# Seven of sixteen heads: the cap of the attention bias as a factor on GpSimd instead of identity products on TensorE

## The reference, cut to what matters

```
slopes = 2 ** (-0.5 * (h + 1))                     # h = 0..15
rel = pos[:, None] - pos[None, :]                  # query minus key
bias = minimum(rel * slopes[h], 8.0)
scores = einsum('bhqd,bhkd->bhqk', q, k) * 8 ** -0.5 + bias
probs = softmax(scores, axis=-1)
out = einsum('bhqk,bhkd->bhqd', probs, v)
```

## Time and profile before

| | us |
|---|---|
| median of 3 runs | 986.8 |
| lowest, highest | 986.79, 990.37 |
| profiled execution | 988.53 |
| span of the profiled execution, first to last instruction | 986.5 |

### The profile page before, as it was taken

How to read it: one execution, slowest core, us unless ns; L and a number is a source line. 1 busy time by engine, 2 the same in 40 slices (tenths; PEclk the granted TensorE clock), 3 DMA queues, 4 the chain that set the end, 5 groups by cost and what they waited for, 6 DMA issues and landing times.

```text
span 986.5 us, 19021 instructions
## 1 busy us (share of the span) xinstructions
PE 783.2 (79%) x5641; PEld 564.8 (57%) x5641; DVE 549.3 (56%) x2190; ACT 395.9 (40%) x947; POOL 357.9 (36%) x543
## 2 busy tenths in 40 slices
PE   0798479999999999952489999999999982038894
PEld 0676355555666677742246676667666651028883
DVE  4688573233322332333588989898987714026672
ACT  0456121222212322210036666766676661025562
POOL 5000517777850134433222423242322102744552
PEclk9999668999999999986569999999999995559997
DMA  9970001111100132303654444444443014111110
GB/s 250 155 221 0 0 1 36 40 41 41 44 0 14 52 112 78 96 30 90 128 106 95 90 108 93 102 83 106 95 85 67 3 45 155 54 53 55 50 50 14
DMA packets 75114, 72.44 MB, mean 73 GB/s; under 512 B 8125, under 2 KB 65680, under 8 KB 72732
## 3 DMA queue, kind: packets, MB, share of 16 engines
q1 hardware_dynamic: 69436, 60.38, 27.3%
q0 software_dynamic: 5600, 11.12, 3.5%
HBM read 43.71 MB, written 27.33 MB: 72 GB/s over the span
## 4 chain that ended last, share of the span: by engine, by line
PE 52%; DVE 18%; issue 12%; DMA 5%; POOL 5%; ACT 3%; DVEq 2%; SPq 2%; POOLq 0%; ACTq 0%
PE bank L1475 10%; PE bank L1476 9%; DVE rt L1065 6%; PE bank L1498 6%; PE bank L1527 4%; PE bank L1617 3%; PE bank L1569 3%; POOL sorted_rows L766 3%; PE bank L1604 3%; PE bank L1599 2%; DMA arena<-arena 2%; SPq L548 1%; DVEq L1180 1%; PE bank L1435 1%; PE bank L1707 1%
## 5 line engine op out<-in xcount | busy, mean ns | idle before, releaser
L1065 DVE CUSTOM_DVE_ANT_0 rt<-bank,alibi 128x256 f32<-128x256 f32 x512 | 192.9, 419 | 44.4 <-PE bank L1569 37.5
L973 DVE TENSOR_TENSOR arena<-arena,bank 128x512 f32<-128x512 f32 (+1 forms) x128 | 75.0, 587 | 187.8 <-ACT arena L1253 187.8
L1280 ACT ACTIVATE arena<-bank 128x512 f32<-128x512 f32 x256 | 150.6, 598 | 55.4 <-PE bank L1604 49.5
L1253 ACT ACTIVATE arena<-bank 128x512 f32<-128x512 f32 (+1 forms) x128 | 66.1, 517 | 202.9 <-PE bank L1476 202.9
L1569 PE MATMUL bank<-arena 72*128 72x256 bf16 x512 | 104.7, 289 | 26.6 <-DMA arena<-qk_parts 13.4
L1599 PE MATMUL bank<-arena 81*128 81x256 bf16 x512 | 117.0, 274 | 8.3 <-ACT arena L1280 4.7
L1475 PE MATMUL bank<-arena 128*128 128x320 f32 (+2 forms) x256 | 115.7, 534 | 7.5 <-DVE arena L973 7.5
L1476 PE MATMUL bank<-arena 128*128 128x320 f32 (+2 forms) x256 | 111.9, 519 | 0.0
L1604 PE MATMUL bank<-arena,ident_b 128*128 128x256 bf16 (+8 forms) x544 | 80.2, 243 | 0.0
L1569 PEld LDWEIGHTS bank<-arena 72*128 72x128 bf16 x512 | 39.0, 102 | 69.4 <-DVE arena L1065 42.8
L1475 PEld LDWEIGHTS bank<-arena 128*128 128x128 f32 x256 | 42.8, 193 | 53.5 <-DVE arena L973 41.1
(11 more groups left out here) (242 smaller groups left out, 1402.9 us busy)
## 6 DMA issues: line engine op xcount, KB each, us to landing
arena<-qk_parts SPq DMA_DIRECT2D x48, 192.0 KB
arena<-qk_parts SPq DMA_DIRECT2D x144, 64.0 KB
qk_parts<-arena SPq DMA_DIRECT2D x16, 384.0 KB, 2.8
back_rows<-empty_row SPq DMA_DIRECT2D x1, 4096.0 KB, 37.8
arena<-back_rows SPq DMA_DIRECT2D x16, 256.0 KB, 3.8
arena<-in_w SPq DMA_DIRECT2D x2, 2048.0 KB, 10.9
xg_rows<-empty_row SPq DMA_DIRECT2D x1, 2580.0 KB, 38.5
arena<-xg_rows SPq DMA_DIRECT2D x8, 322.5 KB, 4.0
```

The source lines that it names most:

```text
L973: nc.vector.tensor_tensor(out, sil[:, k, 0:out.shape[1]], bank[4 + k][:, 0:out.shape[1]], ALU.mult).then_inc(hid_done, 1)
L1065: last = nc.vector.tensor_tensor_reduce(biased[n % 2 * QT + u], bank[n % 2][:, SEQ * u:SEQ * u + SEQ], alibi[:, h, P * (1 - u):P * (1 - u) ...
L1253: nc.scalar.activation(sil[:, k, 0:width], bank[2 + k][:, 0:width], ACT.Silu).then_inc(sil_done, 1)
L1280: nc.scalar.activation(prT3[:, n % (2 * HG)].rearrange("p k t -> p (k t)"), bank[2 + n % 2][:], ACT.Exp).then_inc(exp3_done, 1)
```

## The change

Three things change.

- FULL falls from 4 to 2. Heads 2 to 8 now take their linear bias from the contraction rows, and nothing is added by TensorE for their cap. Instead a table `factor` holds exp(min(8 - slope * rel, 0)) for them, and GpSimd multiplies the exponentials in `prT3` by it (`apply_factor`), from the column `capped_from(h, k)` on. The table is made once: GpSimd writes the corrections, and ScalarE takes the exponential of 128x1792 of it in one instruction ahead of its slot loop.
- `weigh` waits also for `factored` and moves from offset 28 to 30 (WEIGH), its copy from 29 to 31 (KEEP). All that follows on it moves by two slots, with small shifts of single steps. The ring `prT3` grows from 8 to 12 heads.
- GpSimd gets a slot loop. `combine` moves one slot ahead, from -41 and -40 to -42 and -41.

```diff
-FULL = 4
+FULL = 2
+PR = 3 * HG
-COMBINE_0, COMBINE_1, ... = -41, -40, ...
+COMBINE_0, COMBINE_1, ... = -42, -41, ...
-BACK = NH - 1 + EXP_LAG + 5
+FACTOR, WEIGH, KEEP = EXP_LAG + 2, EXP_LAG + 5, EXP_LAG + 6
+BACK = NH - 1 + WEIGH + 2
-RESIDUAL, RESIDUAL_STATS, RESIDUAL_VARIANCE = BACK + 14, BACK + 15, BACK + 19
-NORM_5, TURN_5, COPY_5, ROUTER_5, LOGITS_5 = BACK + 22, BACK + 27, BACK + 28, BACK + 30, BACK + 31
-ROOT_LAG = 5
+RESIDUAL, RESIDUAL_STATS, RESIDUAL_VARIANCE = BACK + 13, BACK + 15, BACK + 20
+ROOT, PARTS_QK, OUTPUT_BIAS, ROOT_5 = VARIANCE + 1, QK_COPY + 1, NORM + 13, BACK + 21
+NORM_5, TURN_5, COPY_5, ROUTER_5, LOGITS_5 = BACK + 24, BACK + 26, BACK + 27, BACK + 29, BACK + 30
...
+def capped_from(h, k):
+    return min((P * k + int(MAX_BIAS / SLOPES[h]) + 1) // 2 * 2, SEQ)
...
+            for h in range(FULL, CLAMPED):
+                f = factor[:, h - FULL, :]
+                strip(nc.gpsimd.tensor_scalar(f, rel[:, P:P + SEQ], -SLOPES[h], MAX_BIAS, ALU.mult, ALU.add))
+                strip(nc.gpsimd.tensor_scalar(f, f, 0.0, None, ALU.min))
...
+        def apply_factor(n):
+            c, h = divmod(n, NH)
+            pool.wait_ge(exp3_done, n + 1)
+            if n == FULL:
+                pool.wait_ge(factor_set, 1)
+            for k in range(QT):
+                first = capped_from(h, k)
+                if first < SEQ:
+                    pr = prT3[:, n % PR, k, first:SEQ]
+                    last = nc.gpsimd.tensor_tensor(pr, pr, factor[:, h - FULL, first - P * k:SEQ - P * k], ALU.mult)
+            last.then_inc(factored, 1)
...
+        act.wait_ge(rows_set, 1)
+        nc.scalar.activation(factor..., factor..., ACT.Exp).then_inc(factor_set, 1)
...
             for k in range(QT):
-                first = bias_from(h, k) if h < CLAMPED else SEQ
-                biases = range(BIAS_PARTS[h]) if first < SEQ else ()
+                biases = range(BIAS_PARTS[h]) if h < FULL else ()
...
         def weigh(g):
             pe.wait_ge(exp3_done, HG * (g + 1))
+            if k * HG < CLAMPED:
+                pe.wait_ge(factored, factors_to(HG * g + HG - 1))
```

More of the change, by code:

```diff
@@ L82, with factors_to @@
 SLOPE_PARTS = [bf16_parts(s) for s in SLOPES]
[L83 to L89, removed]
+BIAS_PARTS = [len([v for v in SLOPE_PARTS[h] if v]) for h in range(FULL)]
+STRIP = [sum(BIAS_PARTS[:h]) for h in range(FULL)]
+FACTORS = CLAMPED - FULL
+def capped_from(h, k):
+    return min((P * k + int(MAX_BIAS / SLOPES[h]) + 1) // 2 * 2, SEQ)
+def factors_to(n):
+    c, h = divmod(n, NH)
+    return FACTORS * c + min(max(h + 1 - FULL, 0), FACTORS)
 def batch_at(slot, offset):
@@ L276, in _build @@
     oT3 = carve([P, SEQ])
-    prT3 = carve([P, 2 * HG, QT, SEQ])
+    prT3 = carve([P, PR, QT, SEQ])
     bn5 = carve([P, 2, QT, 6])
@@ L284, in _build @@
     strip_a = carve([P, sum(BIAS_PARTS[:FULL]), SEQ + P], BF16)
-    strip_b = carve([P, sum(BIAS_PARTS[FULL:]), SEQ], BF16)
+    factor = carve([P, FACTORS, SEQ])
     rel = carve([P, SEQ + P])
@@ L387, in _build @@
     rows_set = sem("rows_set")
+    factor_set = sem("factor_set")
+    factored = sem("factored")
     rows_in = sem("rows_in")
@@ L752, in root5 @@
             nc.gpsimd.tensor_tensor(shift, shift, scale, ALU.mult).then_inc(rstd5_done, 1)
-        root(0)
-        for c in range(BATCH + ROOT_LAG):
-            if alive(c, BATCH):
+        def apply_factor(n):
+            c, h = divmod(n, NH)
+            pool.wait_ge(exp3_done, n + 1)
[7 more added lines that the diff above has]
+            last.then_inc(factored, 1)
+        for slot3 in range(FIRST_SLOT, LAST_SLOT):
+            n = head_at(slot3, FACTOR)
+            if n is not None and FULL <= n % NH < CLAMPED:
+                apply_factor(n)
+            if (c := batch_at(slot3, ROOT)) is not None:
+                root(c)
+            if (c := batch_at(slot3, PARTS_QK)) is not None:
                 parts(c)
-            if alive(c + 1, BATCH):
-                root(c + 1)
-            if alive(c, BATCH):
+            if (c := batch_at(slot3, OUTPUT_BIAS)) is not None:
                 output_bias(c)
-            if alive(c - ROOT_LAG, BATCH):
-                root5(c - ROOT_LAG)
+            if (c := batch_at(slot3, ROOT_5)) is not None:
+                root5(c)
         def send_sorted(i):
@@ L1333, in keep_logits @@
             nc.scalar.activation(lg5[:, QT * e:QT * e + QT, :].rearrange("p t e -> p (t e)"), bank[7][:, SEQ:SEQ + QT * E1], ACT.Copy).then_inc(lg5_done, 1)
+        act.wait_ge(rows_set, 1)
+        nc.scalar.activation(factor.rearrange("p h t -> p (h t)"), factor.rearrange("p h t -> p (h t)"), ACT.Exp).then_inc(factor_set, 1)
         for slot3 in range(FIRST_SLOT, LAST_SLOT):
@@ L1601, in score_turned @@
                 for a in biases:
-                    strip = (strip_a[:, STRIP[h] + a, P * (1 - k):P * (1 - k) + SEQ] if h < FULL else
-                             strip_b[:, STRIP[h] + a, first - P * k:SEQ - P * k])
-                    last = nc.tensor.matmul(out[:, first:SEQ], ident_b[:], strip, start=False, stop=(a == len(biases) - 1))
+                    last = nc.tensor.matmul(out, ident_b[:], strip_a[:, STRIP[h] + a, P * (1 - k):P * (1 - k) + SEQ],
+                                            start=False, stop=(a == len(biases) - 1))
             last.then_inc(st3_mm, 1)
```

36 lines of the change are left out of this document (14 added, 22 removed).

## The result

The changed kernel takes 1006.97 us (median; 1002.27 to 1010.32) where the kernel before took 988.50 on the same chip (986.79 to 990.37). The ratio is 1.0183, 95% interval 1.0134 to 1.0232: slower by 18.5 us, where 15 us less were forecast. The profiled execution had 1010.32 us, its span 1008.4, mean granted clock 0.889 (before 988.53, 986.5, 0.906).

What follows compares the result with a forecast made beforehand. TensorE and VectorE were taken as close to the limit, with a loop through the maxima's DMA setting the new period: 13 x (19.55 - 18.75) = 10.4 plus 5 from the tail, 15.4 us saved, 972 us forecast, range 958 to 983.

Steps and rivals of the forecast that it cites:

- Later steps by two slots: `weigh` and its followers two slots later: priced at nothing, since the slots in the drain are empty.
- The clock was named as a sign: TensorE's granted clock under 1.00 in the changed stage was listed as showing the forecast wrong; no time was given.
- Products removed: TensorE: 26 of 34 identity products in an entry go, cutting its own time by 1.9 us, 18.8 to 16.9.
- The tail: From entry 13 on, nothing is replicated and TensorE bounds; three entries save nearly 1.9 us each: 5 us.
- Combinations moved: VectorE: combination one slot earlier ends before GpSimd's `parts`, taking 1.0 us off VectorE, 18.3 to 17.3.
- GpSimd 12.1 us an entry: Twelve multiplications add 5.8 us to GpSimd's 6.3 in a period; not the bound.
- The heaviest head: GpSimd's multiplication for it takes 1.2 us against a 1.15 us slot, leaving `weigh` two slots to spare; wait costed at nothing.
- New contention: GpSimd's multiplications delay VectorE's normalisation by 0.4 to 0.7 us and maxima splits by 0.4, together 1.0 an entry.
- The loop through the DMA: Maxima queue behind `replicate`, landing 21.8 us after ScalarE's copy; two periods are at least 37.5 us, 18.75 each.
- Rival 3: Normalisation and splits each wait behind a full multiplication: 4.2 us, VectorE 21.5, time 1007; chance 0.10.
- the signs named for "wrong": No maxima wait with period under 18.2; splits and normalisation over 1.5 us more; TensorE waiting for GpSimd; clock under 1.00.

Runs made afterwards that it cites:

- the fifth buffer: The changed kernel with five buffers for VectorE's values instead of four, all offsets kept: 999.94 us, 1.0056 of the kernel before.
- The schedule alone: The kernel before with only the new offsets of `weigh` and its followers and the ring of 12; products kept, no factor, combination unmoved: 1012.95 us, 1.0194.
- Without GpSimd's work: The kernel before with the identity products of heads 2 to 8 left out and nothing in their place: 986.98 us, 0.9951.
- the run without GpSimd's work: The changed kernel with all multiplications on GpSimd left out, GpSimd signalling at once: 1006.61 us, 1.0157 of the kernel before.

## Why the prediction was wrong

- **The step that failed: "At nothing ... Later steps by two slots: in the drain the slots are empty".** I asked who `weigh` would wait for, and where its followers would land at the end. I didn't ask who waits for `weigh` in the steady part. The consumer of `pv3_mm` four entries on is `values`, and its margin was two slots, exactly what the move took. It makes VectorE wait 0.8 us an entry and TensorE 0.8 behind it. An undisturbed entry takes 19.97 us where it takes about 19.0 at the old offset: 0.7 of this 1.0 is that wait, since it goes with the fifth buffer, and 0.3 comes from the two slots in another way that the runs leave open. The schedule alone is 1.0194, and at the old offset all of the loss is gone.
- **The clock was named as a sign, but had no price.** The forecast said that TensorE would be at 0.90 of its stage, waiting. It then worked out no case in which that share costs the clock. On the chip where this was measured it cost 14.9 us (1.0257 against 1.0088). It came with the waits: with the same products at offset 28 or 29 the clock held 1.00 from 560 to 754, and with the fifth buffer 0.99.
- **Products removed, 1.9 us of TensorE an entry:** near. TensorE's busy time of an undisturbed entry fell by 1.4 (19.03 to 17.59). Without GpSimd's work the period falls by 0.6 us (19.6 to 19.0) and the time by 0.5%, with VectorE right behind at 92%.
- **The tail, 5 us from the last three entries:** too high. From the thirteenth first turned score to the sixteenth the kernel before takes 52.8 us, the one without the products 49.9, with `weigh` at 29 51.0 and the changed kernel 53.0.
- **Combinations moved, 1.0 us of VectorE:** right (589 to 346 ns), worth 0.15% or nothing by itself (1.0008 lies in the interval).
- **GpSimd 12.1 us an entry:** right; 11.73 of 20.0. (The heaviest head, put at 1.2 us, is 1.12 by the forecast's own prices.) That `weigh` needn't wait for it was right too, even with no slot moved.
- **New contention 1.0 us an entry:** too high, 0.05 in the changed kernel. At offset 29 normalisation did lose 0.46 us in the pair shown (0.30 by its mean), near the 0.4 to 0.7 taken, and it made no difference to the time. The rule of the Trainium skill ("SBUF — State Buffer", "SBUF: two separate sides"), by which whichever of the two starts first holds the shared port pair for its whole instruction, agrees with 1.06 for 0.60; the splits of the maxima hardly showed it, 243 ns for 193.
- **The loop through the DMA, which set the forecast period of 18.75:** not confirmed. On ScalarE's queue nothing came faster, but neither did the wait go away in those runs. The wait itself is real: with `weigh` at 28 it comes four times from 530 to 760, 3.7 us in all, where the forecast had it in most entries. An undisturbed entry there takes 18.8 to 19.1 us, near the forecast 18.75, with VectorE and TensorE over 90% busy; which of the three sets it isn't separated.
- **The rivals.** Rival 3 has the number, 1007, by a mechanism that the run without GpSimd's work excludes as the main one; that its number came near is luck. It should have been one of many ways to lose, and it got 0.10. Of the signs named for "wrong", the granted clock is the one that came.

## What to carry to other kernels

When a step of a software pipeline moves later, list every semaphore that it raises, find each waiter, and work out the two slots modulo the period, rings included: a margin of two slots used up in full cost more here than the removed work gave. When work is taken off the busiest engine while a wait is added, price the case in which its clock falls. And if a wait is expected to be covered, try first without the slots meant to cover it.

## What the runs showed of the hardware

I hadn't expected that waits of 0.5 to 1.3 us, once an entry, could bring TensorE's clock down to 0.5 for stretches of 3.4 to 13.7 us in an engine that was busy 77% in the 6 us before one fall and 88% over an undisturbed entry, nor that six products more an entry (some 0.6 us by 0.32 for three) hold it: 20.0 us a period with them, 20.9 without on the same chip, 21.6 in the first profile. It doesn't come in every entry: seven of twelve held 1.00 with the same waits. What decides it isn't settled here.
